# Attention scores from split operands: three rounded products in place of one full-precision product, with the rotation reordered by head

## The chip, the cores and the metric

The kernel runs on one core of one Trainium2 chip. The metric is the device time of one execution in microseconds (us). The engines have the names of the profile: PE is TensorE (matmuls), PEld its weight loads, DVE is VectorE, ACT is ScalarE, POOL is GpSimd, SP is SyncE, which starts most DMA transfers.

## The reference

Two transformer layers over x of shape (2, 1024, 256), in float32. The first layer begins with an attention, and only that stage is touched by the change:

```python
q = einsum('btd,hdk->bhtk', x, wq)            # likewise k, v; 2 heads of 128
q = fractional_rope(q, 10000.0)               # first 64 of 128 features are rotated
k = fractional_rope(k, 10000.0)               # the other 64 are kept as they are
q = q * DH ** (-0.5); k = k * DH ** (-0.5)
s = einsum('bhik,bhjk->bhij', q, k)
s = s - 1e+30 * less(i, j)                    # causal
p = softmax(s, axis=-1)
o = einsum('bhij,bhjv->bihv', p, v)
x = x + einsum('bto,od->btd', o.reshape(b, t, NH * DH), wo)
```

The x that goes into q, k and v is first multiplied by a matrix that depends on the batch entry (a weighted sum of 8 matrices under a mask). After the attention come a gated MLP with a chosen expert, a routed layer of 8 experts, and a second layer of MLPs, a gated scan and a last feed-forward layer. These take the span from about 170 us to its end.

## The kernel before

**Tiling.** The 2048 tokens are four chunks of 512 (`CH`). Chunks 0 and 1 are batch entry 0, chunks 2 and 3 are entry 1. For each chunk and head there are four query tiles of 128. Query tile i of an even chunk sees (i + 1) * 128 keys, one of an odd chunk 512 more, so the scores (`S`) are 128 to 1024 wide. In this text S(c,h,i) is the score unit of chunk c, head h, tile i, and likewise T, PV and so on.

**Split operands.** Most products of the kernel are made of three matmuls on rounded operands: a number is kept as `hi` (rounded by a cast to fp32r, mostly by ACT) and `lo` (the difference, mostly by DVE), and hi times hi, hi times lo and lo times hi are added up in PSUM (`products`, L1110 to 1116). The attention's scores (L1190), transposes (L1197) and products with the values (L1206) are exceptions: they run on plain float32 operands.

**The order of the work** is written out by `plan()`: generators append units to one list for each engine, `weave` takes a step of one generator for each step of another, and every engine runs its list in that order. One step of `advance` puts on PE the transposes T of the tile before last, then the score S of a new tile, and after odd tiles the product with the values PV. Around it the other engines run a chain for each tile: DVE's largest value `max` (L1801), ACT's `exp` (L1497), DVE's `recip` (L1806), POOL's `norm` (L2170), PE's T (L1197) and ACT's copy `p_col` (L1506). Beside it runs the preparation of the next chunk, `rotated("k", c)`, `rotated("q", c)` and `value_tiles(c)`:

- `same` (PE, 6 matmuls): the half that is rotated; `same_in` (ACT, L1470) takes it out of PSUM; `swap` (SP, two DMAs) exchanges neighbouring partitions
- `kept` (PE, 6 matmuls): the half that is kept; `skip` (ACT, L1479 and 1480) copies it with its bias to the keys `kT` or queries `qT`, half the partitions for each head
- `cosines`, `sines` (DVE, L1784, L1787), then the sum of both: head 1's 64 partitions by DVE (`rope_1`, L1796), head 0's by POOL (`rope_0`, L2164)
- `v` (PE, two times 12 matmuls) and `v_row` (ACT, L1485)

In chunk 0's stretch DVE also builds the conditioned matrix of batch entry 1 (`half`, L1759, and `half_mask`, L1762), on which the `fold` products (L1160) wait, and behind it POOL issues the indirect loads of the next stage (`ld_pack0`). In chunk 1's stretch the output product of chunk 0 (`out`) is followed by `resid` (DVE, L1815), `x1_hi` (ACT, L1521) and `x1_lo` (DVE, L1819).

**Banks.** PSUM has eight banks. Scores use banks 0 to 3, transposes 4 and 5, and same, kept, v, PV, fold and out take turns on a ring of 2 or 3 banks (6, 7 and sometimes 3). A unit waits until the previous tenant of its bank was read; the table `FREED` says by whom. For `kept` that is ACT's `skip`.

The scores before:

```python
                for w in ("k", "q"):
                    pe.wait_ge(*ready("rope_0", w, c))
                    pe.wait_ge(*ready("rope_1", w, c))
                    pe.wait_ge(*ready("skip", w, c))
                for n0 in range(0, width, CH):
                    n1 = min(n0 + CH, width)
                    pe.matmul(o[:, n0:n1], qT[c % 2][:, h, qs], kT[c // CPB][:, h, n0:n1], start=True, stop=(n1 < width))
                pe.matmul(o[:, width - P:width], ident16[:, :], causal[:, :], start=False, stop=True).then_inc(done)
```

## Time and profile before

| | us |
|---|---|
| median of 3 runs | 930.07 |
| lowest, highest | 929.25, 931.79 |
| profiled execution, whole | 926.78 |
| profiled execution, span of the profile | 925.5 |
| PE busy, share of the span | 911.2, 98% |
| DVE, ACT, POOL busy | 528.7, 444.4, 269.8 |

The rows come from one profiled execution; its own time is 1.28 us longer than the span that the rows cover and 3.3 us below the median. A timeline row is: start in us from the span's beginning, duration in us, engine, line, operation, written tile <- read tiles, size, count and, in brackets, the idle time before it with what ended it. A matmul's duration is its way through the engine, and several are under way at a time, so what one costs PE is the distance between the starts of two, and that is how the prediction reads them. A float32 score matmul has two records. The attention lies between about 29 and 170 us.

### The profile page before, as it was taken

The page shows a single profiled execution, that of the slowest core. Times are in us where ns is not written, and L with a number is a line of the kernel's source. Part 1 is how long each engine was busy: PE and PEld are TensorE (multiplying, and loading weights), DVE is VectorE, ACT ScalarE, POOL GpSimd, SP SyncE. Part 2 cuts the span into 40 slices and gives each one's busy share as a digit, 9 for nine tenths or more (in the row PEclk, how much of TensorE's full clock was granted, in tenths as well). Part 3 has the DMA queues.
Part 4 walks back from the last instruction along what each step waited for, and adds up shares of the span by engine and source line. Part 5 has one row for each costly group of instructions (what it writes and reads, how often), then busy time and mean ns, then how long its engine had stood idle before and what let it go on. Part 6 is the DMA issues. An engine that isn't in the chain of part 4 may idle for free.

```text
span 925.5 us, 13114 instructions
## 1 busy us (share of the span) xinstructions
PE 911.2 (98%) x4859; PEld 767.9 (83%) x4859; DVE 528.7 (57%) x975; ACT 444.4 (48%) x827; POOL 269.8 (29%) x242
## 2 busy tenths in 40 slices
PE   8999999999999999999999999999999999999998
PEld 4768868887799999998888888888888888888886
DVE  6754454578757766785665564333333335688544
ACT  3665566434355455572343343343343442345775
POOL 1533321310475765653400152041140230010000
PEclk9999999999999999999999999999999999999999
DMA  8030001220445343432503013003003011000011
GB/s 301 30 114 23 24 1 69 104 81 28 121 129 157 125 126 126 126 125 77 180 18 148 12 24 137 0 1 137 1 8 129 1 55 83 1 0 1 1 46 46
DMA packets 22192, 67.47 MB, mean 73 GB/s; under 512 B 4514, under 2 KB 11954, under 8 KB 19314
## 3 DMA queue, kind: packets, MB, share of 16 engines
q1 hardware_dynamic: 16546, 40.15, 11.9%
q0 software_dynamic: 5440, 26.50, 9.9%
q8 instruction: 39, 0.64, 0.3%
q14 instruction: 23, 0.19, 0.1%
q10 hardware_dynamic: 144, 0.00, 0.0%
HBM read 55.09 MB, written 9.45 MB: 70 GB/s over the span
## 4 chain that ended last, share of the span: by engine, by line
PE 89%; DVE 4%; issue 2%; DMA 2%; ACT 2%; POOL 1%; SPq 0%; ACTq 0%; DVEq 0%; POOLq 0%
PE banks L1112 18%; PE banks L1114 18%; PE banks L1113 18%; PE banks L1365 5%; PE banks L1367 5%; PE banks L1366 5%; PE banks L1206 3%; PE banks L1190 3%; PE banks L1404 2%; PE banks L1403 2%; PE banks L1197 2%; PE banks L1417 1%; PE banks L1416 1%; PE banks L1160 1%; DMA weight_stage<-in_cond_w 1%
## 5 line engine op out<-in xcount | busy, mean ns | idle before, releaser
L1112 PE MATMUL banks<-input_hi,mlp_hi 128*128 128x512 f32 x376 | 147.6, 392 | 0.0
L1114 PE MATMUL banks<-input_hi,mlp_lo 128*128 128x512 f32 x376 | 146.4, 389 | 0.0
L1113 PE MATMUL banks<-input_lo,mlp_hi 128*128 128x512 f32 x376 | 146.4, 389 | 0.0
L1631 ACT CAST hidden_hi<-hidden 128x512 fp32r<-128x512 f32 x96 | 59.6, 621 | 158.6 <-DVE hidden L2048 107.5
L2237 POOL TENSOR_TENSOR mlp_lo<-weight_stage,mlp_hi 128x768 fp32r<-128x768 f32 x32 | 59.1, 1846 | 172.4 <-ACT mlp_hi L1609 172.4
L2054 DVE TENSOR_TENSOR hidden_lo<-hidden,hidden_hi 128x512 fp32r<-128x512 f32 x96 | 66.4, 692 | 61.7 <-ACT hidden_hi L1631 61.4
L2048 DVE SCALAR_TENSOR_TENSOR hidden<-banks,L_expert_weight,gelu 128x512 f32<-128x512 f32 x64 | 48.0, 750 | 83.6 <-PE banks L1114 80.5
L1625 ACT ACTIVATE gelu<-banks 128x512 f32<-128x512 f32 x96 | 57.4, 598 | 71.2 <-PE banks L1114 63.5
L1114 PEld LDWEIGHTS banks<-input_hi,mlp_lo 128*128 128x128 f32 x376 | 70.6, 188 | 14.8
L1113 PEld LDWEIGHTS banks<-input_lo,mlp_hi 128*128 128x128 f32 x376 | 70.6, 188 | 14.4
L1112 PEld LDWEIGHTS banks<-input_hi,mlp_hi 128*128 128x128 f32 x376 | 70.6, 188 | 14.2
L1112 PE MATMUL banks<-expert_in_hi,ffn_w_hi 128*128 128x256 f32 (+1 forms) x256 | 79.8, 312 | 0.1
L1114 PE MATMUL banks<-expert_in_hi,ffn_w_lo 128*128 128x256 f32 (+1 forms) x256 | 78.9, 308 | 0.0
L1113 PE MATMUL banks<-expert_in_lo,ffn_w_hi 128*128 128x256 f32 (+1 forms) x256 | 78.8, 308 | 0.0
L1365 PE MATMUL banks<-hidden_hi,mlp_hi 128*128 128x512 f32 x192 | 75.1, 391 | 0.0
L1367 PE MATMUL banks<-hidden_hi,mlp_lo 128*128 128x512 f32 x192 | 74.8, 390 | 0.0
L1366 PE MATMUL banks<-hidden_lo,mlp_hi 128*128 128x512 f32 x192 | 74.7, 389 | 0.0
L2197 POOL TENSOR_TENSOR ffn_w_lo<-weight_stage,ffn_w_hi 128x512 fp32r<-128x512 f32 x42 | 54.5, 1300 | 32.5 <-ACT ffn_w_hi L1568 32.5
L1975 DVE TENSOR_TENSOR expert_hidden_lo<-hidden,expert_hidden_hi 128x256 fp32r<-128x256 f32 (+1 forms) x64 | 46.1, 720 | 25.9 <-ACT expert_hidden_hi L1587 25.2
L2209 POOL DMA_INDIRECT gathered<-routed_input,token_of_slot x40 | 39.7, 992 | 69.5 <-DMA routed_input<-x_rows 53.3
L2050 DVE TENSOR_TENSOR hidden<-banks,gelu 128x512 f32<-128x512 f32 x32 | 22.1, 691 | 48.4 <-PE banks L1114 48.1
L1112 PEld LDWEIGHTS banks<-expert_in_hi,ffn_w_hi 128*128 128x128 f32 x256 | 48.4, 189 | 0.7 <-issue 0.6
(350 smaller groups left out, 2148.8 us busy)
## 6 DMA issues: line engine op xcount, KB each, us to landing
weight_stage<-in_packF SPq DMA_DIRECT2D x8, 1536.0 KB, 7.0
weight_stage<-in_shared SPq DMA_DIRECT2D x2, 3072.0 KB, 11.2
expert_output<-y_rows SPq DMA_DIRECT2D x40, 128.0 KB, 1.8
weight_stage<-in_cond_w SPq DMA_DIRECT2D x4, 512.0 KB, 5.3
residual<-in_xT SPq DMA_DIRECT2D x4, 512.0 KB, 10.7
first_half_swapped<-first_half SPq DMA_DIRECT2D x16, 128.0 KB, 2.0
routed_input<-x_rows SPq DMA_DIRECT2D x16, 128.0 KB, 1.7
weight_stage<-in_ffn_w SPq DMA_DIRECT2D x2, 1024.0 KB, 7.1
```

The lines of the kernel that those rows point to most:

```text
L1112: pe.matmul(o, wh, dh, start=(i == 0), stop=False)
L1113: pe.matmul(o, wh, dl, start=False, stop=False)
L1114: last = pe.matmul(o, wl, dh, start=False, stop=(i == len(terms) - 1))
L1365: pe.matmul(o, dh[:, i, ms], hiD[r][:, :], start=first, stop=False)
L1366: pe.matmul(o, dh[:, i, ms], loD[r][:, :], start=False, stop=False)
L1367: last = pe.matmul(o, dl[:, i, ms], hiD[r][:, :], start=False, stop=final)
L1625: act.activation(gelu_t[n % 2][:, :], bank(("gu", *key, 0)), ACT.Gelu_apprx_tanh, bias=0.0).then_inc(done)
L1631: act.copy(hiD[n % 4][:, :], prod_t[n % 2][:, :]).then_inc(done)
L2048: dve.scalar_tensor_tensor(prod_t[m % 2][:, :], o, wsel[:, n // 3, n % 3:n % 3 + 1], gelu_t[m % 2][:, :], ALU.mult, ALU.mult).then_inc(done)
L2054: dve.tensor_tensor(loD[m % 4][:, :], prod_t[m % 2][:, :], f(hiD[m % 4][:, :]), ALU.subtract).then_inc(done)
L2197: pool.tensor_tensor(lo, src, f(hi), ALU.subtract).then_inc(done)
L2237: pool.tensor_tensor(wDl[s][:, qs], stage[:, qs], f((wDh if n else wDl)[s][:, qs]), ALU.subtract).then_inc(done)
```

## The change

It touches only the attention, in four ways.

1. **Scores.** Keys and queries are kept as hi and lo (`kH`, `kL`, `qH`, `qL`), and each score is three matmuls on rounded operands for each chunk of keys: q_hi with k_hi, q_hi with k_lo, q_lo with k_hi. In the chunk of the diagonal each is at least 256 wide. The first matmul waits only for the hi parts (`turn_hi`, `skip`), the second for the lo parts.
2. **Splitting.** `rope_1` (DVE) now adds all 128 partitions in place, in `cos_t`. `turn_hi` (ACT, two for each of the eight key or query units, 64 x 512) rounds it, and the rest is made by POOL for one head (`rope_0`, now a subtraction) and by DVE for the other (`rope_lo`). `skip` (ACT) writes the hi of the kept half, `skip_lo` (DVE, two for each unit, 64 x 512, reads PSUM) its lo, and a bank of `kept` is now free only after the second `skip_lo`.
3. **Slots.** Keys and values are held for three chunks in turn and not for all four; the matrices that the fold reads share memory with what `ld_pack0` loads, which therefore has three more waits.
4. **Order.** `rotated(c)` treats keys and queries in overlapping steps, each operation one step behind its input; the first `same` of chunk 1 stands ahead of S(0,0,0), the values' copies of chunk 0 stand behind the rotation on ACT, and `later_input(3)` comes after `rotated(2)`.

```diff
@@ -184,29 +185,71 @@
     def first_rotated():
         for w in ("q", "k"):
             product("out", "kept", w, 0)
-            act.append(("skip", w, 0))
-        run(value_tiles(0))
         for w in ("k", "q"):
             dve.append(("sines", w, 0))
+            dve.append(("rope_1", w, 0))
             pool.append(("rope_0", w, 0))
-        for w in ("k", "q"):
-            dve.append(("rope_1", w, 0))
-
-    def rotated(w, c):
+        for h in range(NH):
+            for w in ("q", "k"):
+                act.append(("skip", w, 0, h))
+                act.append(("turn_hi", "k" if w == "q" else "q", 0, h))
+                dve.append(("skip_lo", w, 0, h))
+            dve.append(("rope_lo", "k" if h else "q", 0))
+        run(value_tiles(0))
+
+    in_bank = []
+
+    def swapped(w, c):
         product("out", "same", w, c)
         act.append(("same_in", w, c))
         sp.append(("swap", w, c))
-        yield
+
+    def kept(w, c):
         product("out", "kept", w, c)
-        act.append(("skip", w, c))
+        for h in range(NH):
+            act.append(("skip", w, c, h))
         dve.append(("cosines", w, c))
-        yield
-        if c == 1:
-            yield
+        in_bank.append((w, c))
+
+    def rest_of_kept():
+        while in_bank:
+            unit = in_bank.pop()
+            for h in range(NH):
+                dve.append(("skip_lo", *unit, h))
+
+    def turning(w, c):
         dve.append(("sines", w, c))
         dve.append(("rope_1", w, c))
+
+    def rests(w, c):
+        dve.append(("rope_lo", w, c))
         pool.append(("rope_0", w, c))
-        yield
+
+    def rotated(c):
+        swapped("k", c)
+        yield
+        swapped("q", c)
+        yield
+        kept("k", c)
+        yield
+        rest_of_kept()
+        turning("k", c)
+        kept("q", c)
+        yield
+        rest_of_kept()
+        for h in range(NH):
+            act.append(("turn_hi", "k", c, h))
+        turning("q", c)
+        yield
+        rests("k", c)
+        for h in range(NH):
+            act.append(("turn_hi", "q", c, h))
+        yield
+        tiles_left = value_tiles(c)
+        next(tiles_left)
+        rests("q", c)
+        yield
+        yield from tiles_left
 
...
                 project.append(u[0])
             yield
         for c in chunks:
+            rest_of_kept()
             project.pop(0)
             product("out", "out", c, 0)
...
@@ -301,14 +345,16 @@
     act.append(("wo_hi",))
     pool.append(("wo_lo",))
     share_banks(False)
-    run(weave(weave(attention(0), chain(rotated("k", 1), rotated("q", 1), value_tiles(1))), chain([None] * 3, conditioned_half(4, G))))
+    coming = rotated(1)
+    next(coming)
+    run(weave(weave(attention(0), coming), chain([None] * 3, conditioned_half(4, G))))
     dve.append(("half_mask",))
     pool.append(("ld_pack0", 0))
     share_banks(True)
     fold = folded(1)
-    run(weave(attention(1), chain(some(fold, 2), later_input(2), fold, later_input(3), rotated("k", 2), rotated("q", 2), value_tiles(2))))
+    run(weave(attention(1), chain(some(fold, 2), later_input(2), fold, rotated(2), later_input(3))))
     share_banks(False)
-    run(weave(attention(2), chain(rotated("k", 3), rotated("q", 3), value_tiles(3))))
+    run(weave(attention(2), rotated(3)))
     share_banks(True)
     run(weave(attention(3), split0(0), 3))
...
@@ -783,6 +829,8 @@
         return ("gelu1" if key[2] == 0 else "prod2", *key[:2])
     if kind == "inv":
         return ("slots",)
+    if kind == "kept":
+        return ("skip_lo", *key, NH - 1)
...
+    qH = [sb("queries_hi", [P, NH, CH], F32R) for _ in range(2)]
+    qL = [sb("queries_lo", [P, NH, CH], F32R) for _ in range(2)]
+    second = sb("values", [P, QT, D])
     scored_top = top[0]
-    vR.append(sb("values", [P, TPB, D]))
+    vR = [sb("values", [P, QT, D]), second, sb("values", [P, QT, D])]
     ptT = [sb("probT", [P, TPB, PAIR]) for _ in range(2)]
-    woS, woH, woL = sb("out_weights", [P, KD, D]), sb("out_weights_hi", [P, KD, D], F32R), sb("out_weights_lo", [P, KD, D], F32R)
...
                 for w in ("k", "q"):
-                    pe.wait_ge(*ready("rope_0", w, c))
-                    pe.wait_ge(*ready("rope_1", w, c))
-                    pe.wait_ge(*ready("skip", w, c))
-                for n0 in range(0, width, CH):
-                    n1 = min(n0 + CH, width)
-                    pe.matmul(o[:, n0:n1], qT[c % 2][:, h, qs], kT[c // CPB][:, h, n0:n1], start=True, stop=(n1 < width))
+                    pe.wait_ge(*ready("turn_hi", w, c, h))
+                    pe.wait_ge(*ready("skip", w, c, h))
+                spans = [(c - 1, 0, CH)] if c % CPB else []
+                spans.append((c, width - (i + 1) * P, max((i + 1) * P, PAIR)))
+                q_hi, q_lo = qH[c % 2][:, h, qs], qL[c % 2][:, h, qs]
+                for of, n0, n in spans:
+                    pe.matmul(o[:, n0:n0 + n], q_hi, kH[of % SLOTS][:, h, 0:n], start=True, stop=False)
+                    if of == spans[0][0]:
+                        for w in ("k", "q"):
+                            pe.wait_ge(*ready("rope_0" if h == head_of_pool(w, c) else "rope_lo", w, c))
+                            pe.wait_ge(*ready("skip_lo", w, c, h))
+                    pe.matmul(o[:, n0:n0 + n], q_hi, kL[of % SLOTS][:, h, 0:n], start=False, stop=False)
+                    pe.matmul(o[:, n0:n0 + n], q_lo, kH[of % SLOTS][:, h, 0:n], start=False, stop=(of != c))
                 pe.matmul(o[:, width - P:width], ident16[:, :], causal[:, :], start=False, stop=True).then_inc(done)
             elif kind == "T":
...
-                w, c = key
+                w, c, h = key
                 o, bs = bank(("kept", w, c)), fbias[:, 1:2] if w == "q" else fbias[:, 3:4]
-                if w == "q" and c >= 2:
+                if w == "q" and c >= 2 or c >= SLOTS:
                     act.wait_ge(*ready("S", c - 2, NH - 1, QT - 1))
                 act.wait_ge(*ready("bias_in"))
                 act.wait_ge(*ready("kept", w, c))
-                dst = qT[c % 2][:, :, :] if w == "q" else kT[c // CPB][:, :, sl(c % CPB)]
-                act.activation(dst[0:P // 2, 1, :], o[0:P // 2, :], ACT.Identity, bias=bs[0:P // 2, :])
-                act.activation(dst[P // 2:P, 0, :], o[P // 2:P, :], ACT.Identity, bias=bs[P // 2:P, :]).then_inc(done)
+                dst, _ = turned_halves(w, c)
+                act.activation(dst[kept_rows(h), h, :], o[kept_rows(h), :], ACT.Identity, bias=bs[kept_rows(h), :]).then_inc(done)
+            elif kind == "turn_hi":
+                w, c, h = key
+                n = rope_no[w, c] % 2
+                if w == "q" and c >= 2 or c >= SLOTS:
+                    act.wait_ge(*ready("S", c - 2, NH - 1, QT - 1))
+                act.wait_ge(*ready("rope_1", w, c))
+                dst, _ = turned_halves(w, c)
...
                 n = rope_no[w, c] % 2
-                if w == "q" and c >= 2:
-                    dve.wait_ge(*ready("S", c - 2, NH - 1, QT - 1))
                 dve.wait_ge(*ready("cosines", w, c))
                 dve.wait_ge(*ready("sines", w, c))
-                dst = qT[c % 2][:, :, :] if w == "q" else kT[c // CPB][:, :, sl(c % CPB)]
-                dve.tensor_tensor(dst[P // 2:P, 1, :], cos_t[n][P // 2:P, :], sin_t[n][P // 2:P, :], ALU.add).then_inc(done)
+                dve.tensor_tensor(cos_t[n][:, :], cos_t[n][:, :], sin_t[n][:, :], ALU.add).then_inc(done)
+            elif kind == "skip_lo":
+                w, c, h = key
+                o, bs = bank(("kept", w, c)), fbias[:, 1:2] if w == "q" else fbias[:, 3:4]
+                hi, lo = turned_halves(w, c)
+                rs = kept_rows(h)
+                dve.wait_ge(*ready("skip", w, c, h))
+                dve.scalar_tensor_tensor(lo[rs, h, :], o[rs, :], bs[rs, :], f(hi[rs, h, :]), ALU.add, ALU.subtract).then_inc(done)
+            elif kind == "rope_lo":
+                w, c = key
+                n, h = rope_no[w, c] % 2, 1 - head_of_pool(w, c)
+                hi, lo = turned_halves(w, c)
+                rs = turned_rows(h)
+                dve.wait_ge(*ready("turn_hi", w, c, h))
+                dve.tensor_tensor(lo[rs, h, :], cos_t[n][rs, :], f(hi[rs, h, :]), ALU.subtract).then_inc(done)
...
@@ -2156,12 +2247,15 @@
             elif kind == "rope_0":
                 w, c = key
                 n = rope_no[w, c] % 2
-                if w == "q" and c >= 2:
-                    pool.wait_ge(*ready("S", c - 2, NH - 1, QT - 1))
-                pool.wait_ge(*ready("cosines", w, c))
-                pool.wait_ge(*ready("sines", w, c))
-                dst = qT[c % 2][:, :, :] if w == "q" else kT[c // CPB][:, :, sl(c % CPB)]
-                pool.tensor_tensor(dst[0:P // 2, 0, :], cos_t[n][0:P // 2, :], sin_t[n][0:P // 2, :], ALU.add).then_inc(done)
+                hi, lo = turned_halves(w, c)
+                h = head_of_pool(w, c)
+                rs = turned_rows(h)
+                pool.wait_ge(*ready("turn_hi", w, c, h))
+                if h:
+                    pool.wait_ge(*ready("rope_0", "k", 0))
+                pool.tensor_tensor(lo[rs, h, :], cos_t[n][rs, :], f(hi[rs, h, :]), ALU.subtract).then_inc(done)
+                if h:
+                    pool.wait_ge(*ready("rope_0", w, c))
...
@@ -2172,6 +2266,9 @@
                 pool.wait_ge(*ready("pick0"))
                 pool.wait_ge(*ready("cw"))
                 pool.wait_ge(*ready("half_mask"))
+                pool.wait_ge(*ready("bias_in"))
+                pool.wait_ge(*ready("fold", 0, KD - 1, 1))
+                pool.wait_ge(*ready("wo_lo"))
                 for b in range(B):
                     pool.indirect_dma_start(by_row[b][:, :], None, A["down_by_row"], bass.IndirectOffsetOnAxis(ap=dyn0[:, b:b + 1], axis=0)).then_inc(ld["by_row"], 16)
                 pool.indirect_dma_start(stage[:, 0:PK0], None, A["pack0"], bass.IndirectOffsetOnAxis(ap=dyn0[:, 0:1], axis=0)).then_inc(ld["pack0_0"], 16)
```

DVE's list in chunk 0's stretch, between the third score's `max` and the next. Names: softmax_stats is what `max` and `recip` write, times_cos and times_sin what `cosines` and `sines` write. Before, from `recip` of tile 0 on:

```order
L1806 RECIPROCAL softmax_stats_117<-softmax_stats_117 128x1
L1784 TENSOR_TENSOR times_cos_95<-first_half_91,rope_cos_89 128x512
L1801 TENSOR_REDUCE softmax_stats_117<-banks 128x1
L1806 RECIPROCAL softmax_stats_117<-softmax_stats_117 128x1
L1801 TENSOR_REDUCE softmax_stats_117<-banks 128x1
L1806 RECIPROCAL softmax_stats_117<-softmax_stats_117 128x1
L1787 TENSOR_TENSOR times_sin_97<-first_half_swapped_93,rope_sin_90 128x512
L1796 TENSOR_TENSOR keys_103<-times_cos_95,times_sin_97 64x512
```

In the change, from the same place:

```order
L1897 RECIPROCAL softmax_stats_120<-softmax_stats_120 128x1
L1864 TENSOR_TENSOR times_cos_95<-first_half_91,rope_cos_89 128x512
L1892 TENSOR_REDUCE softmax_stats_120<-banks 128x1
L1897 RECIPROCAL softmax_stats_120<-softmax_stats_120 128x1
L1880 SCALAR_TENSOR_TENSOR keys_lo_104<-banks,folded_bias_118,keys_hi_101 64x512 x2
L1867 TENSOR_TENSOR times_sin_97<-first_half_swapped_93,rope_sin_90 128x512
L1873 TENSOR_TENSOR times_cos_95<-times_cos_95,times_sin_97 128x512
L1864 TENSOR_TENSOR times_cos_96<-first_half_92,rope_cos_89 128x512
L1892 TENSOR_REDUCE softmax_stats_120<-banks 128x1
L1897 RECIPROCAL softmax_stats_120<-softmax_stats_120 128x1
```

Before, `max` of tile 3 and `recip` of tile 2 (the second TENSOR_REDUCE and the third RECIPROCAL) stood directly behind `recip` of tile 1; now five rotation operations (two `skip_lo`, `sines`, `rope_1`, `cosines`) stand between them.

PE's list in chunk 1's stretch, around the score S(1,1,1) with its 768 keys. Before (L1197 are the transposes, L1190 the score, L1206 is PV(1,0,1)):

```order
L1197 MATMUL banks<-identity_55,weight_stage_54 128x128 x7
L1190 MATMUL banks<-keys_103,queries_106 128x512
L1190 MATMUL banks<-keys_103,queries_106 128x256
L1191 MATMUL banks<-causal_mask_57,identity_bf_8_56 128x128
L1206 MATMUL banks<-probT_109,values_107 128x256 x5
L1206 MATMUL banks<-probT_109,values_107 128x128
```

In the change:

```order
L1269 MATMUL banks<-identity_55,weight_stage_54 128x128 x7
L1256 MATMUL banks<-keys_hi_100,queries_hi_107 128x512
L1261 MATMUL banks<-keys_lo_103,queries_hi_107 128x512
L1262 MATMUL banks<-keys_hi_100,queries_lo_109 128x512
L1256 MATMUL banks<-keys_hi_101,queries_hi_107 128x256
L1261 MATMUL banks<-keys_lo_104,queries_hi_107 128x256
```

Two float32 matmuls have become six rounded ones (the sixth and the causal mask follow), and behind them `kept` of the next queries now comes ahead of PV(1,0,1), which takes the bank that `kept` of the keys has filled.

## Rows read from the trace of the kernel before

**Rows 1.** The page: busy time by engine; the granted clock of PE in 40 slices.
```profile
PE 911.2 (98%) x4859; PEld 767.9 (83%) x4859; DVE 528.7 (57%) x975; ACT 444.4 (48%) x827; POOL 269.8 (29%) x242
...
PEclk9999999999999999999999999999999999999999
```
**Rows 2.** Windows: busy us (x instructions) of PE, PEld, DVE, ACT, POOL; clock; DMA.
```profile
29.40:49.90 20.50, 19.25 (x103) 14.37 (x103) 13.85 (x29) 13.15 (x34) 10.17 (x10) 1.00 0.07 26
49.90:92.00 42.10, 41.53 (x202) 30.67 (x203) 22.31 (x37) 25.56 (x51) 14.99 (x14) 1.00 0.22 76
```
**Rows 3.** Timeline of PE: T(0,0,2), the first fold, out of chunk 0, a T of chunk 3.
```profile
37.54 0.49 PE L1197 MATMUL banks<-identity,weight_stage 128*128 128x128 f32 x3
...
49.90 1.53 PE L1160 MATMUL banks<-ery_key_value_weights,cond_weight 128*128 128x384 f32 x4 [0.64 <-DVE cond_weight L1762]
...
69.00 0.50 PE L1112 MATMUL banks<-input_hi,out_weights_hi 128*128 128x512 f32 x1 [0.43 <-ACT first_half L1470]
...
125.21 0.33 PE L1197 MATMUL banks<-identity,probabilities 128*128 128x128 f32 x1 [0.34 <-ACT probT L1506]
```
**Rows 4.** Timeline of PE: scores and the causal mask behind them, 128, 640, 1024 keys.
```profile
90.81 0.39 PE L1190 MATMUL banks<-keys,queries 128*128 128x128 f32 x2
91.04 0.22 PE L1191 MATMUL banks<-causal_mask,identity_bf 128*128 128x128 bf16 x1
...
118.66 1.32 PE L1190 MATMUL banks<-keys,queries 128*128 128x512 f32 x4
119.81 0.22 PE L1191 MATMUL banks<-causal_mask,identity_bf 128*128 128x128 bf16 x1
...
141.42 1.88 PE L1190 MATMUL banks<-keys,queries 128*128 128x512 f32 x4
143.14 0.22 PE L1191 MATMUL banks<-causal_mask,identity_bf 128*128 128x128 bf16 x1
```
**Rows 5.** Timeline of PE: products of rounded operands behind PV, 512 and 256 wide.
```profile
76.33 0.48 PE L1112 MATMUL banks<-input_hi,folded_hi 128*128 128x512 f32 x1
76.64 0.39 PE L1113 MATMUL banks<-input_lo,folded_hi 128*128 128x512 f32 x1
76.87 0.39 PE L1114 MATMUL banks<-input_hi,folded_lo 128*128 128x512 f32 x1
...
87.20 0.36 PE L1176 MATMUL banks<-folded_hi,input_hi 128*128 128x256 f32 x1
87.41 0.28 PE L1177 MATMUL banks<-folded_lo,input_hi 128*128 128x256 f32 x1
87.52 0.28 PE L1178 MATMUL banks<-folded_hi,input_lo 128*128 128x256 f32 x1
```
**Rows 6.** Timeline of DVE: the rotation of chunk 0, a reciprocal, the mask.
```profile
24.46 1.28 DVE L1787 TENSOR_TENSOR times_sin<-first_half_swapped,rope_sin 128x512 f32<-128x512 f32 x2
...
27.36 1.78 DVE L1796 TENSOR_TENSOR queries<-times_cos,times_sin 64x512 f32<-64x512 f32 x1
...
35.66 0.15 DVE L1806 RECIPROCAL softmax_stats<-softmax_stats 128x1 f32<-128x1 f32 x1
...
49.07 0.68 DVE L1762 TENSOR_TENSOR cond_weight<-cond_weight,cond_mask 128x512 f32<-128x512 f32 x1
```
**Rows 7.** Timeline of POOL: the rotation of chunk 0's queries.
```profile
26.85 1.73 POOL L2164 TENSOR_TENSOR queries<-times_cos,times_sin 64x512 f32<-64x512 f32 x1
```
**Rows 8.** Groups by form, DVE, 29 to 147 us: a sum that reads PSUM.
```profile
L1815 DVE TENSOR_TENSOR residual<-banks,residual 128x512 f32<-128x512 f32 x6 | 4.2, 692 | 4.6 <-PE banks L1114 4.6
```
**Rows 9.** Timeline of ACT: `skip` of a head, a rounding copy from SBUF.
```profile
24.90 0.68 ACT L1479 ACTIVATE queries<-banks,folded_bias 64x512 f32<-64x512 f32 x1 [0.95 <-PE banks L1114]
...
29.83 0.62 ACT L1455 CAST out_weights_hi<-out_weights 128x512 fp32r<-128x512 f32 x1
```
**Rows 10.** Timeline of ACT and DVE: `x1_hi` and `x1_lo` of chunk 0.
```profile
71.42 1.05 ACT L1521 CAST input_hi<-residual 128x1024 fp32r<-128x1024 f32 x1 [2.47 <-DVE residual L1815]
```
```profile
72.50 1.23 DVE L1819 TENSOR_TENSOR input_lo<-residual,input_hi 128x1024 fp32r<-128x1024 f32 x1 [1.11 <-ACT input_hi L1521]
```

38 lines of the change are left out of this document (26 added, 12 removed).

## The prediction

> **What bounds the kernel now.** I read the page first: PE is busy for 98% of the span, and the granted clock is full in all forty slices [rows 1], so nothing is to be had from the clock (the rows read here lie on its level of 2.4 GHz), and a microsecond of PE work removed is a microsecond of time, as long as nobody lets PE wait. The attention has that form too, but less safely. In chunk 0's stretch, 29.4 to 49.9 us, PE is busy for 19.25 of 20.5 us and DVE for 13.85; from 49.9 to 92 it is 41.53 and 22.31 of 42.1 [rows 2]. DVE is thus the next engine in chunk 0, with 6.65 us of slack, and that slack lies in small gaps. Of PE's waits the ones that matter are 0.64 us before the first fold, for DVE's mask, 0.43 us before the output of chunk 0, and 0.34 us before a transpose in chunk 3 [rows 3]. From 170 us on the change touches nothing; what comes there starts from what PE has finished, so I let it shift as a whole.
>
> **PE work.** A score costs from its first record to the causal mask behind it: 0.23 us for 128 keys, 1.15 for 640, 1.72 for 1024 [rows 4]. That is about 0.21 us for each 128 keys on a full 512 (0.86), and 0.23 for the first. So four tiles of an even chunk and head cost about 0.23 + 0.43 + 0.65 + 0.86 = 2.17 us, and of an odd one 1.15 + 1.34 + 1.53 + 1.72 = 5.74 us. The new scores are the same kind of matmul as the split products: 0.23 us from start to start at 512 columns and 0.11 to 0.12 at 256, but the first of a group that follows float32 work costs 0.31 and 0.21 [rows 5]. In nearly all cases a transpose or a PV stands ahead of a score, so I charge each score one dear first matmul, and 0.17 for each 384-wide one. Even: 0.45 twice (the 128-key tile is 256 wide now), 0.60, 0.77, together 2.27 us, which is 0.10 more than before. Odd: 0.77 for the old chunk each time, plus 0.36, 0.36, 0.51, 0.69, together 5.00 us, which is 0.74 less. Each kind comes four times (two chunks, two heads). The odd chunks give back 3.0 us, chunk 2 costs 0.2, and chunk 0's 0.2 is inside the next term.
>
> The Trainium skill has a rule on this ("FP8 and Floating Point Precision", TensorE Precision Notes): true FP32 goes through the array four times, reduced precision once. By that three passes replace four. Read with this kernel's rows it would give a quarter of the scores' 4 * (2.17 + 5.74) = 31.6 us, that is 7.9 us; the rows say 2.6 us net, because of the 256 minimum and the dear first matmul. The sum goes by the rows.
>
> **Chunk 0: DVE.** Ahead of S(0,0,0) DVE does two sines and two sums from 24.46 to 29.14 us; the sums take 1.78 us beside POOL's [rows 6, 7]. It now does two sines (1.28), two sums over all partitions that mostly miss POOL (about 0.7 each), four `skip_lo` and two `rope_lo`. The trace has no `skip_lo`; between a sine's 0.64 and 1.78 us I take 0.69, the addition that reads PSUM [rows 8]. A `rope_lo` reads two tiles of SBUF beside POOL's subtraction: between 0.64 and 1.78 I take 1.0. That is 1.3 + 1.4 + 2.8 + 2.0 = 7.5 us, so DVE gets to its first `max` at about 32.0 in place of 29.1. PE does not idle for that, since `same` of chunk 1 (1.4 us) now stands ahead and S(0,0,0) starts at about 30.4. In the stretch itself DVE gets four more `skip_lo` and two more `rope_lo`, 4.8 us. 32.0 + 13.85 + 4.8 gives 50.7 us for the end of the mask if DVE never waits, against 49.75 (49.07 + 0.68) [rows 6]: 0.9 us late at least. It will wait: the second `max` needs S(0,0,1), the cosines need ACT's `same_in`, the `skip_lo` need ACT's `skip`. And the order makes PE wait too. `recip` of tile 2, done at 35.8 before [rows 6], now stands behind `max` of tile 3 and that behind two `skip_lo`, sines, a sum and cosines, 3.3 us of work that starts at about 35.7. With POOL's `norm` behind it T(0,0,2), at 37.54 before [rows 3], comes at about 40.5, and PE stands for some 3 us, the largest new gap I expect. Walking the lists on with these durations, the mask ends at 51.3 to 52.5 and the first fold starts 2.2 us later than its 49.90. Bounds: 0.9 us if DVE is never kept waiting, 5 us if it can use only half of its 6.65 us of slack (4.8 + 2.9 of added work and delay less 3.3, and 0.6 for contention).
>
> The Trainium skill tells where such contention ends ("SBUF — State Buffer", Who interferes with whom): a DVE instruction with two SBUF inputs blocks against a POOL instruction that reads SBUF, one with a single SBUF input does not. The trace agrees on the sums (1.78 beside 1.73 us of POOL, 0.64 for a sine alone). By it `skip_lo` is safe and the sums, `half` and `rope_lo` are not.
>
> **ACT.** Sixteen `turn_hi` of about 0.62 us [rows 9]; `skip` keeps its 0.68 each. In chunk 0's stretch ACT rises from 13.15 by 2.5 of 20.5 us [rows 2], and ahead of it by another 2.5, which delays the values' copies, the exp of tile 0 and POOL's `wo_lo`. PE would wait for that only where it already waits for DVE, so it costs nothing of its own; its cover is DVE's lateness, and without that it would cost up to 1 us.
>
> **Chunk 1: the bank.** PV(1,0,1) takes the bank of `kept` of the keys, which was free after ACT's `skip` and now is free after DVE's second `skip_lo`. From the end of `out`: the residual's sum 0.69, `x1_lo` after `x1_hi` 1.05 + 1.23, cosines 0.64, the `max` of S(1,1,1) about 1, two `skip_lo` 1.4: DVE frees it after some 6.2 us [rows 8, 10]. PE needs it after `kept`, seven transposes, S(1,1,1) and `kept` of the queries, 1.4 + 0.8 + 1.1 + 1.4 = 4.7 us. That is a wait of up to 1.5 us; I take 1.4. On the other side the 0.43 us before `out` [rows 3] goes, since `same` of the queries now gives ACT time. Net +1.0. Bounds: -0.4 (DVE gets there in time) and +2.
>
> **Chunks 2 and 3.** Chunk 2's new DVE work (six operations, 4.8 us) lies beside long PE work (four rotation products, two of values, two of `out`), and the bank is needed only at `v`; nothing. In chunk 3 a T waited 0.34 us for the softmax chain [rows 3], which does not get shorter, while PE gets there sooner. Of the 1.5 us that chunk 3 gives, I let 0.4 be lost (bounds 0 and 0.8).
>
> **Other moves, at nothing.** SP's swaps keep their number, and the later ones have whole PE products to land in. POOL has as many operations as before; its `rope_0` of the keys stands one `norm` later. `ld_pack0` waits in addition for things that are done before the mask, but as the mask is late, its three issues are too, and the `norm` behind them; that is inside the 2.2 us. The slots' waits are on scores and PVs of two chunks ago, done long before.
>
> **The sum**: -3.0 + 0.2 + 2.2 + 1.0 + 0.4 = +0.8 us. The profiled execution would go from 926.8 to 927.6; it stands 3.3 us below the median, so 930.07 becomes 930.9.
>
> **The rivals.** A change of 0.3%, 2.8 us, is about what a measurement of this kernel can tell from none.
>
> - *Faster: the overlap does what it is for.* DVE's gaps are filled, the first fold comes 0.9 us late at most, no bank wait: -3.0 + 0.2 + 0.9 - 0.4 = -2.3 us. With the dear first matmul hidden as well, because the weights of the next are loaded under the scores' long ones (0.08 us for each of 32 scores, 2.6 us), -4.9, 925.2 us. For it: ordinary spacing of 0.23 inside a group. Against: the rows behind PV, and T before nearly each score. A quarter off the scores, as by the page, would be 922 us before waits.
> - *Slower: DVE and POOL block each other in chunk 0.* The sums, `half` and `rope_lo` each wait for a POOL subtraction of 1.7 us, the mask ends 5 us late, the folds and the loads with it, and chunk 1 adds its 2 us: -2.8 + 5 + 2 + 0.8 = +5, 935 us. It decides from the point where DVE has under 2 us of idle left between 29 and 50 us. For it: the 1.78 us row; against: the subtractions are on 64 partitions as before and no more numerous.
> - *The scores are not cheaper at all* (each of the three matmuls as dear as half a float32 one): 1.5 times 31.6 is 16 us more. The rows for the same kind of operands exclude it nearly; 2%.
>
> **Chances.** My forecast with its bounds, 0.5; the faster rival past 0.3%, 0.23; the slower one past 0.3%, 0.27, which includes the last. Leaving out 2 in 10, the range is 926.0 to 936.0.
>
> **What would show it.** PE's busy time falls by 2 to 4 us, with a score of 1024 keys at 1.46 us from start to mask and one of 128 keys at 0.45. A gap of 2 to 4 us before T(0,0,2) near 38 us, released by POOL. The first fold at 51 to 53 us, released by DVE's mask. A gap of about 1 us before PV(1,0,1). From 170 us on all stretches as long as before. Wrong it would be if the first fold starts before 50.5 or after 54 us, if the score of 1024 keys takes 1.72 us, or if the part behind 170 us changes its length by over 1 us.

## The result and the profile after

The changed kernel takes 940.54 us (median of 4 executions, 939.83 to 942.43), the kernel before 930.93 us beside it (929.25 to 932.46): a ratio of 1.0107, 95% interval 1.0088 to 1.0126. Repeated later beside others it was 1.0097 (1.0080 to 1.0113). I had forecast 930.9 us in a range of 926.0 to 936.0. The change costs 9 to 10 us.

The page, busy time by engine, answers to [rows 1]: PE's work rose by 3.6 us though the scores got cheaper, since part of it runs at a lower clock; in a second profile of the same kernel, at full clock, it is 910.1 us, 1.1 less than before.

```profile
PE 914.8 (97%) x4907; PEld 779.0 (83%) x4907; DVE 543.8 (58%) x999; ACT 452.6 (48%) x843; POOL 266.5 (28%) x242
```

Windows of the changed kernel, columns as in [rows 2]; the first ends, as there, at the first fold. The stretch of chunk 0 is 25.78 us long and not 20.5; PE is idle for 4.4 us of it, and DVE works 22.41 us. The next has 3.7 us of idle PE.

```profile
29.40:55.18 25.78, 21.36 (x121) 17.67 (x119) 22.41 (x40) 18.40 (x43) 10.91 (x12) 0.93 0.06 22
55.18:97.40 42.22, 38.54 (x201) 30.74 (x202) 25.60 (x40) 25.15 (x49) 13.64 (x13) 1.00 0.22 75
```

The timeline of PE, the larger waits up to chunk 3 (in brackets the idle time and its releaser). They answer to [rows 3], where the largest is 0.64 us.

```profile
42.43 0.52 PE L1269 MATMUL banks<-identity,weight_stage 128*128 128x128 f32 x3 [2.76 <-POOL weight_stage L2264]
...
55.18 0.56 PE L1225 MATMUL banks<-ery_key_value_weights,cond_weight 128*128 128x384 f32 x1 [0.18 <-DVE cond_weight L1842]
...
69.78 0.49 PE L1177 MATMUL banks<-input_hi,folded_hi 128*128 128x512 f32 x1 [1.08 <-DVE folded_lo L1851]
...
83.62 2.65 PE L1278 MATMUL banks<-probT,values 128*128 128x256 f32 x12 [1.55 <-DVE keys_lo L1880]
...
100.84 0.47 PE L1177 MATMUL banks<-input_hi,folded_hi 128*128 128x512 f32 x1 [1.85 <-issue]
...
121.36 0.47 PE L1177 MATMUL banks<-input_hi,out_weights_hi 128*128 128x512 f32 x1 [1.66 <-DVE times_cos L1873]
...
137.75 0.33 PE L1269 MATMUL banks<-identity,probabilities 128*128 128x128 f32 x1 [0.61 <-ACT probT L1586]
```

In order these are T(0,0,2), the first fold, `same k 2`, PV(1,0,1), `same k 3`, `out 1 0` and a T of chunk 3. With four of 0.4 to 0.55 us between 32 and 61 us and one of 0.41 before values at 96.21, PE's waits up to chunk 3 come to some 12 us, against some 3 before.

The scores themselves, to be held against [rows 4]: 1024 keys from 89.37 to the mask at 90.84, 1.47 us; 128 keys from 98.32 to 98.76, 0.44 us.

```profile
89.37 0.47 PE L1256 MATMUL banks<-keys_hi,queries_hi 128*128 128x512 f32 x1
...
90.84 0.23 PE L1263 MATMUL banks<-causal_mask,identity_bf 128*128 128x128 bf16 x1
...
98.32 0.36 PE L1256 MATMUL banks<-keys_hi,queries_hi 128*128 128x256 f32 x1
...
98.76 0.23 PE L1263 MATMUL banks<-causal_mask,identity_bf 128*128 128x128 bf16 x1
```

Why T(0,0,2) waits is told by DVE's timeline and POOL's (rows of POOL behind them). The scores of tile 2 are long there, but `recip` of tile 2 stands behind `skip_lo` of k 1 (L1880), sines, a sum, cosines and the `max` of tile 3, as forecast, and is done at 41.6, where it was 35.8 before [rows 6].

```profile
37.40 1.53 DVE L1880 SCALAR_TENSOR_TENSOR keys_lo<-banks,folded_bias,keys_hi 64x512 fp32r<-64x512 f32 x2
38.86 0.67 DVE L1867 TENSOR_TENSOR times_sin<-first_half_swapped,rope_sin 128x512 f32<-128x512 f32 x1
39.64 0.69 DVE L1873 TENSOR_TENSOR times_cos<-times_cos,times_sin 128x512 f32<-128x512 f32 x1
40.24 0.69 DVE L1864 TENSOR_TENSOR times_cos<-first_half,rope_cos 128x512 f32<-128x512 f32 x1
40.85 0.68 DVE L1892 TENSOR_REDUCE softmax_stats<-banks 128x1 f32<-128x512 f32 x1
41.45 0.15 DVE L1897 RECIPROCAL softmax_stats<-softmax_stats 128x1 f32<-128x1 f32 x1
```
```profile
41.70 0.58 POOL L2264 TENSOR_SCALAR weight_stage<-weight_stage,softmax_stats 128x384 f32<-128x384 f32 x1 [3.76 <-DVE softmax_stats L1897]
```

The new work of DVE by form, 22 to 125 us (count | busy us, mean ns). Of the low parts, `skip_lo` is L1880 and `rope_lo` L1887: 12.0 and 8.3 us. POOL's sums of before are gone from the path, and DVE's sum over all partitions (0.69 us) misses POOL.

```profile
L1880 DVE SCALAR_TENSOR_TENSOR queries_lo<-banks,folded_bias,queries_hi 64x512 fp32r<-64x512 f32 x8 | 6.0, 750 | 0.3
L1880 DVE SCALAR_TENSOR_TENSOR keys_lo<-banks,folded_bias,keys_hi 64x512 fp32r<-64x512 f32 x8 | 6.0, 749 | 0.2
L1873 DVE TENSOR_TENSOR times_cos<-times_cos,times_sin 128x512 f32<-128x512 f32 x8 | 5.5, 692 | 0.8
L1887 DVE TENSOR_TENSOR queries_lo<-times_cos,queries_hi 64x512 fp32r<-64x512 f32 x4 | 4.6, 1150 | 0.2
...
L1887 DVE TENSOR_TENSOR keys_lo<-times_cos,keys_hi 64x512 fp32r<-64x512 f32 x4 | 3.7, 922 | 0.1
```

### The profile page after: what moved, and what is told of

The parts are those of the page before. It is cut to its first block, busy times and chain, and to the rows that moved or that the text cites. A ratio compares the mean times of both kernels' runs of the same rounds, so it can differ in the third digit from the quotient of the medians.

```text
span 941.2 us, 13294 instructions
## 1 busy us (share of the span) xinstructions
PE 914.8 (97%) x4907; PEld 779.0 (83%) x4907; DVE 543.8 (58%) x999; ACT 452.6 (48%) x843; POOL 266.5 (28%) x242
## 4 chain that ended last, share of the span: by engine, by line
PE 88%; DVE 6%; issue 2%; ACT 2%; DMA 1%; POOL 0%; SPq 0%; DVEq 0%; ACTq 0%; POOLq 0%
PE banks L1177 19%; PE banks L1179 19%; PE banks L1178 19%; PE banks L1437 5%; PE banks L1439 5%; PE banks L1438 5%; PE banks L1278 2%; PE banks L1476 2%; PE banks L1475 2%; PE banks L1488 1%; PE banks L1489 1%; PE banks L1269 1%; PE banks L1353 1%; DMA weight_stage<-in_cond_w 1%; DVE softmax_stats L1892 1%
## 5 line engine op out<-in xcount | busy, mean ns | idle before, releaser
L2066 DVE TENSOR_TENSOR expert_hidden_lo<-hidden,expert_hidden_hi 128x256 fp32r<-128x256 f32 (+1 forms) x64 | 44.2, 691 | 26.3 <-ACT expert_hidden_hi L1667 24.6
```

## The experiments

Three theories stood after the result: single steps stand in the wrong place (**order**); the low parts' work is too much for DVE (**work**); PE's lower granted clock behind the waits (**clock**). Each ratio below is to the kernel before, measured beside it with five rounds; 0.001 is 0.93 us, and the intervals reach 0.001 to 0.002 to either side.

**The changed kernel again.**

> The changed kernel itself, beside the others of this group, since the kernel before took 926.97 us beside the last four and 930.93 beside the first measurement. Expected: the same ratio as first measured, 1.0107 within its interval of 1.0088 to 1.0126.

1.0097. Its profile has the same waits at the same places, but the clock stays full (windows of PE: busy, clock, DMA; first this run, then the changed kernel as first profiled).

```profile
40.00:50.00 10.00, 7.09 (x49) 1.00 0.00 1
100.00:110.00 10.00, 9.93 (x56) 1.00 0.15 55
```
```profile
40.00:50.00 10.00, 7.57 (x46) 0.83 0.00 1
100.00:110.00 10.00, 9.16 (x40) 0.83 0.15 53
```

In the first profile matmuls at half the rate follow the wait of 2.76 us at 42.43 and that of 1.85 us at 100.84, which puts them on the 1.2 GHz level for a while; here the same waits have nothing behind them. Between T(0,0,2) and the first fold both profiles take the same 12.7 us (42.43 to 55.18, 41.68 to 54.42), because PE here stands 1.24 us for POOL at 48.63 instead. Between `same k 3` and `out 1 0` it is 20.52 against 18.90 us: there the clock costs 1.6 us. The six executions of this run took 937.02 and 938.18 us at a mean granted clock of 1.000, 937.78 at 0.998, and 939.24 to 941.28 at 0.994 to 0.995; but one of the first measurement took 940.25 at 1.000. So the lower clock has a part in the ratios, of a size that was not isolated.

```profile
48.63 0.30 PE L1269 MATMUL banks<-identity,probabilities 128*128 128x128 f32 x1 [1.24 <-POOL probabilities L2264]
...
118.97 0.47 PE L1177 MATMUL banks<-input_hi,out_weights_hi 128*128 128x512 f32 x1 [1.69 <-DVE times_cos L1873]
```

A measure of the attention alone is the time from the first `kept` product of chunk 0 to the last `out` product that reads the high parts of both operands. Here are the two rows before, then those of this run, both at full clock: 145.35 and 154.34 us, 9.0 us more. The first profile of the changed kernel, with its lower clock, has 156.00.

```profile
22.98 0.69 PE L1112 MATMUL banks<-input_hi,folded_hi 128*128 128x512 f32 x1
...
168.33 0.39 PE L1112 MATMUL banks<-input_hi,out_weights_hi 128*128 128x512 f32 x1
```
```profile
23.28 0.69 PE L1177 MATMUL banks<-input_hi,folded_hi 128*128 128x512 f32 x1
...
177.62 0.39 PE L1177 MATMUL banks<-input_hi,out_weights_hi 128*128 128x512 f32 x1
```

What lies behind the last `out` does not go with the kernel but with the group of runs, each group having been made on a chip of its own: 756.2 to 757.7 us in the eight profiles of two groups, 759.3 to 761.5 in the seven of the other two. The medians of the kernel before differ likewise, 925.96 and 926.97 us against 930.27 and 931.38. Spans of single profiles from different chips can thus differ by some 4 us without any change.

**Order: the input of chunk 3 early.**

```
-    run(weave(attention(1), chain(some(fold, 2), later_input(2), fold, rotated(2), later_input(3))))
+    run(weave(attention(1), chain(some(fold, 2), later_input(2), fold, later_input(3), rotated(2))))
```

> Of the changed kernel, one move is undone: in the stretch of chunk 1 the input of chunk 3 is made ahead of the rotation of chunk 2, as before the change. Theory (the move, which I had costed at nothing, makes the products of `same k 3` wait for `x0_lo 3`, and TensorE then runs at its lower clock for a while): the wait of 1.85 us at 100.84 goes and most of the 10 us of lower clock behind it with it, so 2.5 to 3.5 us less than the changed kernel's 940.5: 937.0 to 938.0. Rival (the time is only moved: chunk 2's rotation is late instead, or the wait at `out 1 0` grows): 940 to 941.

1.0099, so the rival. The wait at `same k 3` is gone, and these two stand in the timeline of PE instead: the bank of `kept` of k 2 comes free later, and an `o_lo` holds the values.

```profile
84.91 0.50 PE L1177 MATMUL banks<-input_hi,folded_hi 128*128 128x512 f32 x1 [2.73 <-DVE keys_lo L1880]
...
97.54 0.39 PE L1241 MATMUL banks<-folded_hi,input_hi 128*128 128x256 f32 x1 [1.83 <-DVE input_lo L1902]
```

**Order: `recip` earlier on DVE** (a pass over DVE's finished list moves each `recip` up to two operations behind its row's `max`).

> Of the changed kernel, only VectorE's order is changed: each `recip` stands at most two other operations behind its row's `max`, instead of up to six, so that GpSimd gets its normalization earlier; no work is added or removed. Theory (in chunk 0 `recip 0 0 2` stands behind the low parts of k 1, GpSimd idles for it, and T(0,0,2) waits 2.76 us, with TensorE at its lower clock for some us behind): the wait shrinks below 1 us and the clock stays, 2 to 4 us less than 940.5: 936.5 to 938.5, with the first fold at 52 to 53.5 instead of 55.18. Rival (VectorE is simply full in this stretch, so whatever is put first delays the rest): `same k 2` and the mask wait longer by what T(0,0,2) gains, 939.5 to 941.

1.0136: the rival, and more than it wanted (939.5 to 941 us, up to 1.011). T(0,0,2) waits 0.52 us, and within 12 us PE waits three times elsewhere, first for the bank of `kept` of q 1.

```profile
39.80 0.52 PE L1285 MATMUL banks<-identity,weight_stage 128*128 128x128 f32 x3 [0.52 <-POOL weight_stage L2280]
...
43.93 0.89 PE L1294 MATMUL banks<-probT,values 128*128 128x256 f32 x4 [1.60 <-DVE queries_lo L1896]
...
48.88 0.33 PE L1285 MATMUL banks<-identity,probabilities 128*128 128x128 f32 x1 [1.58 <-ACT probT L1602]
...
51.33 1.04 PE L1294 MATMUL banks<-probT,values 128*128 128x256 f32 x3 [1.21 <-ACT values L1581]
```

**Order: `o_lo 1 1 3` first.**

```
+    dve.remove(("o_lo", 1, 1, 3))
+    dve.insert(dve.index(("sines", "q", 3)), ("o_lo", 1, 1, 3))
```

> The changed kernel with one operation of VectorE moved: `o_lo 1 1 3` stands ahead of `sines q 3` and `rope_1 q 3`, not behind them. Theory (`out 1 0` waits 1.69 us because its last input stands two operations behind, and nothing hides it): 1.2 to 1.5 us less than the changed kernel, ratio 1.0082, with the wait at `out 1 0` under 0.5 us. Rival (the rotation of q 3 is late in its place, or a later wait takes it back): 1.0097, as the changed kernel.

1.0111. `out 1 0` follows after 0.24 us, and the values behind it wait for ACT, whose copy stands behind `turn_hi` of the rotation that is now later: 1.07 of the 1.69 us come back. That the ratio is no lower than 1.0097 is within the intervals.

```profile
117.60 0.47 PE L1179 MATMUL banks<-input_hi,out_weights_hi 128*128 128x512 f32 x1 [0.24 <-issue]
...
121.65 0.39 PE L1243 MATMUL banks<-folded_hi,input_hi 128*128 128x256 f32 x1 [1.07 <-ACT values L1567]
```

**Both repairs.**

> The changed kernel with both single repairs that keep its result: the input of chunk 3 ahead of chunk 2's rotation, and `o_lo 1 1 3` ahead of `sines q 3`. Each alone left the time where it was (1.0099 and 1.0111 against 1.0097 and 1.0107). Theory (VectorE's total work up to the end of chunk 2's stretch decides, so a repaired wait comes back at the next place): 1.008 to 1.011. Rival (the waits are separate, and the two repairs save 1.9 and 1.7 us together): 1.006 or less.

1.0096: they do not add up.

**Order: the old one, and other work moved out of chunk 0.** In the first, k and q are rotated one after the other as before, with `turn_hi` and the rests one step behind. In the second, the last four `half` and the mask go behind `later_input(2)` and `later_input(3)` into chunk 1.

> The new arithmetic in the old order: k and q of a chunk are rotated one after the other, as before the change, no rotation is begun ahead of the attention loop, and the input of chunk 3 is early; of the change's own order only this stays, that the high and low parts are formed one step behind the products of the rotation. Theory that the new order is at fault: under 936. Theory that the split's own work on VectorE and GpSimd is at fault in chunk 0, in whatever order: 937 to 942, without the wait for the input of chunk 3.

> Of the changed kernel, work that is not the split's is moved out of the full stretch: the last four `half` steps and the mask of the second folded weights (five operations of VectorE) are made beside chunk 1 and not beside chunk 0, the inputs of chunks 2 and 3 ahead of the fold; nothing is added or removed. Theory (VectorE is too full between 30 and 60 us, and has room between 60 and 80): the waits at PV(1,0,1) and `same k 3` shrink, 3 to 6 us less than the changed kernel: ratio 1.004 to 1.008. Rival (chunk 2's rotation, now one step later, is late for chunk 2's scores): 1.010 or more, with a wait of some us at S(2,0,0).

1.0155 and 1.0150. The first is above both theories (under 936 us, or 937 to 942, which is up to 1.012): in the old order PE waits 3.40 us for POOL's `norm` at 49.26 and 3.09 us before `out 1 0` at 123.77. The new order is thus the better one for the new arithmetic. The second falls as a remedy: T(0,0,2) waits 2.76 us as before, since the `half` steps stand behind it, and where the fold was there is now a wait of 3.20 us for the softmax chain; the folds had been PE's cover. Chunk 2's first score also waits, 0.81 and 0.98 us, which is the rival's sign. That DVE has room later was right and no help.

**Clock: filler at T(0,0,2).**

```
+    spin(10, 4)
+    pe.insert(pe.index(("T", 0, 0, 2, 0)), pe.pop())
```

> The changed kernel with ten filler products (bf16, 512 columns, about 2.1 us together, result not used) on TensorE ahead of T(0,0,2), where it waits 2.76 us. Theory (the wait itself costs 2.76 us, and the lower clock behind it another 1.5; the filler takes away only the second): granted clock 1.00 between 40 and 50 us, 1.3 to 1.7 us less than the changed kernel, ratio about 1.009. Rival (the lower clock there is not owed to the wait, or what TensorE loses there it would have waited anyway): the same as the changed kernel.

1.0122: nothing gained, the rival. The clock is at 1.00 from 40 to 50 us, as it also is in some profiles without filler; what was lost there PE would have waited. This prices the clock at one place only: the four executions with the filler still have a mean clock of 0.996 to 0.998.

**Work: the low parts left out, or formed and not read.** Edits: no `skip_lo`, `rope_lo`, `rope_0` in the lists; or only this in the scores:

```
-                q_hi, q_lo = qH[c % 2][:, h, qs], qL[c % 2][:, h, qs]
+                q_hi, q_lo = qH[c % 2][:, h, qs], qH[c % 2][:, h, qs]
...
-                    pe.matmul(o[:, n0:n0 + n], q_hi, kL[of % SLOTS][:, h, 0:n], start=False, stop=False)
+                    pe.matmul(o[:, n0:n0 + n], q_hi, kH[of % SLOTS][:, h, 0:n], start=False, stop=False)
```

> Of the changed kernel, the low parts of the rotated queries and keys are left out (VectorE's `skip_lo` and `rope_lo`, GpSimd's `rope_0`); the three products stay, all of them on the high parts, so TensorE's work is the same and the scores lack the two correction products' content. Theory (what the split costs is its additional work on VectorE and GpSimd, and the waits that this makes): waits at T(0,0,2), PV(1,0,1) and `out 1 0` go, that for the input of chunk 3 stays with its lower clock (3.5 us): 930.9 - 2.8 + 3.5 = 931.6, within 930 to 934. Rival (the three products themselves are dearer than priced somewhere, or the order of the steps is at fault and not the work): 937 or more.

> The low parts are formed as in the changed kernel, with the same work on VectorE and GpSimd, and they free the banks as there; but the scores' three products all read the high parts, so the scores lack the correction products' content and TensorE waits for no low part. Leaving the low parts out altogether gave 1.0025 of the kernel before. Theory (the cost is that the work fills VectorE in chunk 0 and holds what stands behind it, recips, banks, `o_lo`): 1.009 to 1.012, as the changed kernel. Rival (the cost is that TensorE waits for the low parts to be ready): 1.002 to 1.005.

1.0025 (1.0014 to 1.0035) and 1.0122 (1.0107 to 1.0136). This pair decides: the loss comes with the work, and it stays whole when nobody reads the result. Of the attention alone, at full clock, the profiles say the same: 145.23 us without low parts, 154.20 with low parts that nobody reads, 154.34 with all as changed. (That 1.0122 is above 1.0097 is thus not found in the attention; the intervals overlap.) In this order PE does not wait for low parts, it waits for what stands behind them; in two of the reordered kernels above a score did wait for POOL's low part, 0.87 us in the old order and 0.98 with the `half` steps moved. The rows, without low parts and then with unread ones:

```profile
23.30 0.69 PE L1171 MATMUL banks<-input_hi,folded_hi 128*128 128x512 f32 x1
...
168.53 0.39 PE L1171 MATMUL banks<-input_hi,out_weights_hi 128*128 128x512 f32 x1
```
```profile
23.23 0.69 PE L1177 MATMUL banks<-input_hi,folded_hi 128*128 128x512 f32 x1
...
177.43 0.39 PE L1177 MATMUL banks<-input_hi,out_weights_hi 128*128 128x512 f32 x1
```

**Which part of the work.**

> As the kernel that forms the low parts and does not read them (1.0122 of the kernel before; the changed kernel itself 1.0097), but without `skip_lo`, the low parts of the rows that are not rotated: four VectorE operations of 0.76 us in each chunk, which also hold the bank of `kept`. The scores again lack the correction products' content. Leaving out all low parts gave 1.0025. Theory (it is VectorE's time and the held bank): `skip_lo` has the larger part, about 3.1 of 5.3 us in a chunk, so two thirds of the 0.0075 to 0.0097 go: 1.004 to 1.006. Rival (the cost is GpSimd's `rope_0` and what VectorE loses beside it): 1.008 to 1.010.

> The other half alone: `skip_lo` stays, and `rope_lo` (VectorE, 0.69 us) and `rope_0` (GpSimd, 1.29 us), the low parts of the rotated rows, are left out; nothing reads low parts. Theory (VectorE's time and the held bank): a third goes, 1.007 to 1.009. Rival (GpSimd's share and the contention, where a VectorE operation of 0.67 us takes 1.6 to 1.7 beside it): 1.003 to 1.005.

1.0033 and 1.0088. `skip_lo` carries 8.3 us of the difference to 1.0122 (6.0 us of that to 1.0097), more than its share of the time and more than forecast; the rotated rows' low parts carry 1 to 3 us, POOL's operations among them. The two do not simply add up: taken out one at a time they give 8.3 and 3.2 us, together 9.0. Without `skip_lo` the attention takes 146.66 us at full clock, 7.5 less than the 154.20, and without the rest too it takes another 1.4 less.

```profile
23.64 0.69 PE L1174 MATMUL banks<-input_hi,folded_hi 128*128 128x512 f32 x1
...
170.30 0.39 PE L1174 MATMUL banks<-input_hi,out_weights_hi 128*128 128x512 f32 x1
```

**`skip_lo`: its time, or the bank it holds.**

```
-  lo[rs, h, :], o[rs, :], bs[rs, :], f(hi[rs, h, :])
+  lo[rs, h, :], ropeC[rs, sl(c % CPB)], bs[rs, :], f(hi[rs, h, :])     (bank free after skip)
+  lo[rs, h, 0:1], o[rs, 0:1], bs[rs, :], f(hi[rs, h, 0:1])             (bank as before)
```

> As the kernel that forms the low parts and does not read them, but `skip_lo` takes its first operand from a table in SBUF (wrong values, same size, same place in the order) and the bank of `kept` is free once `skip` has read it. Theory (VectorE's time, what stands behind it in its queue): as with the bank held, 1.009 to 1.012. Rival (the held bank, by which PV(1,0,1) waits 1.55 us and others with it): 1.5 to 3 us less, 1.006 to 1.008.

> As the kernel that forms the low parts and does not read them, but `skip_lo` works on one column and not on 512: it stands in the same place and frees the bank of `kept` at the same point of VectorE's order, and takes a small part of its 0.75 us. Theory (VectorE's time is the cost): close to the kernel without `skip_lo`, 1.003 to 1.005. Rival (the bank held until VectorE comes to it is the cost): 1.007 to 1.010.

The first, 1.0134, is inconclusive: with both operands in SBUF `skip_lo` took 0.93 us and not 0.75, which adds nearly 3 us of DVE work; the wait at PV(1,0,1) is gone there, but T(0,0,2) waits 4.20 us. The second, 1.0044, speaks for DVE's time: the same places in the queue and the same bank, but 0.22 us each, and most of the cost is gone. The wait at PV(1,0,1) falls from 1.55 to 0.49 us with it, so it is mostly that time seen at a bank. What the held bank would cost by itself was not isolated, since DVE also comes to it sooner here. DVE by form, 22 to 125 us:

```profile
L1879 DVE SCALAR_TENSOR_TENSOR queries_lo<-banks,folded_bias,queries_hi 64x1 fp32r<-64x1 f32 x8 | 1.7, 217 | 0.3
```

**What is left without low parts.**

> The kernel without any low parts (1.0025 in the new order) in the old order of the steps, with the input of chunk 3 early; the scores lack the correction products' content. Theory (the new order costs some 4 us by itself, for T(0,0,2) waits 1.8 us, `same k 3` 1.85 and `same k 2` 1.08 there although no low part is made; what is left is the 2.8 us that TensorE saves): 0.997 to 0.999. Rival (the waits come from the additional high parts on ScalarE, in whatever order): 1.002 to 1.005.

1.0022 (1.0010 to 1.0034), where the order theory wanted 0.999 or less: by its number the rival. Without low parts both orders are thus 2 us slower than before, though their scores are cheaper: summed over the 32 scores, from first record to causal mask, they take 31.5 us before and 29.1 us without low parts. But the granted clock is not the same on both sides, a third explanation beside order and high parts. Without low parts it is 0.996 to 0.999 in the new order and 0.994 to 0.998 in the old one, while the kernel before beside them has 0.999 to 1.000 and 0.996 to 1.000. In the new order the execution with the highest clock took 926.48 us, below the 926.97 of the kernel before; the other seven took 928.19 to 929.68. Its attention, all at full clock, takes 145.23 us against 145.35. There the waits, 1.81 us at T(0,0,2), 1.08 at `same k 2` and 1.85 at `same k 3` among them, use up the 2.4 us of the scores and no more; the further 2 us of the ratio may be the clock's, which was not tested. In the old order the waits are released by ACT's high parts and the chain behind them; from 50 to 60 us its granted clock is 0.66.

```profile
51.22 0.48 PE L1244 MATMUL banks<-keys_hi,queries_hi 128*128 128x512 f32 x1 [1.92 <-ACT queries_hi L1546]
...
53.37 0.98 PE L1213 MATMUL banks<-ery_key_value_weights,cond_weight 128*128 128x384 f32 x1 [0.78 <-DVE cond_weight L1829]
```

The releasers point to the sixteen `turn_hi` on ACT (0.61 us each); what they cost by themselves was not tried. No version with the right scores beat the kernel before.

## Why the prediction was wrong

The prediction had the change at +0.8 us. At full clock the attention grew by 9.0 us: 4.2 us up to the first fold, where 2.2 were forecast, and 4.8 us from the first fold to the last `out` (118.43 to 123.20 us), where -1.4 was. What failed is the pricing of DVE's added work: at 2.2 us in chunk 0, and at nothing behind it except for one bank.

- **PE work: right for a score, too high in the sum.** 1.47 and 0.44 us against 1.46 and 0.45 forecast. But the 32 scores fell from 31.5 to 29.4 us, 2.1 and not 2.6: four scores of an odd chunk cost 5.66 us before and 5.07 after, where I had 5.74 and 5.00 from interpolated rows. PE's busy time at full clock fell by 1.1 us, under the 2 to 4 that I named. The quarter off that I had read from the Trainium skill's four passes for true FP32 ("FP8 and Floating Point Precision", TensorE Precision Notes) is not seen; it is 7%.
- **"DVE gets to its first `max` ...": nearly right.** 32.9 us in the repeated profile against 32.0, and S(0,0,0) waits 0.43 us where I had none. **The gap before T(0,0,2): right.** 2.76 us, released by POOL, where I had said some 3. The durations held: `skip_lo` 0.75 (0.69 taken), `rope_lo` 0.69 alone and 0.92 to 1.15 on average (1.0 taken).
- **"The first fold starts 2.2 us later": wrong.** It starts at 55.18 against 49.90; of these 5.28 us 1.05 lie ahead of the rotation of chunk 0 (the first `kept` product at 24.03 against 22.98, a matter of the execution: 23.28 when repeated). 4.2 us are the change's. My walk let DVE catch up behind T(0,0,2); but PE and DVE wait there for each other by turns, and the next waits (1.24, 0.52, 0.50 us in the repeated profile) each add. From 29 to 50 us DVE has 2.2 us of idle left, where it had 6.9; the slower rival was to hold from under 2.
- **Chunk 1's bank: right in size,** 1.55 against 1.4 (the terms for DVE add up to 6.0 us, not to the 6.2 written), and the 0.43 us before `out` went as said; but I did not see that `folded_lo` delays `same k 2` by 1.08 us.
- **"Other moves, at nothing": wrong.** The input of chunk 3 went behind chunk 2's rotation, and the text did not even name it; `same k 3` waits 1.85 us for it (`x0_hi` on ACT at 98.43, `x0_lo` on DVE until 100.7). Undoing it gained nothing, so its true price beside the rest is near nought: the step failed in the reading of the trace, not in the sum.
- **"Chunk 2's new DVE work lies beside long PE work; nothing": wrong.** `out 1 0` waits 1.66 us, since its `o_lo` stands behind two `skip_lo`, sines (1.74 us beside POOL) and a sum. This and the last are one error: I priced DVE stage by stage by slack, while the queue carries the delay into the next stage, and each repair only moves the place where it shows. The runs put in its place a price of 12.0 us of `skip_lo` at 6 to 8 us.
- **"ACT ... costs nothing of its own ... up to 1 us": open.** Without the low parts PE's saving of 2.4 us is used up even at full clock, but order and high parts were not separated.
- **From 170 us on: no effect of the change shown.** The part behind the last `out` is 761.16 and 759.31 us in the two profiles against 757.21, more than the 1 us that I named as a sign of being wrong; but it goes with the group of runs and its chip, and so does a wait of 1.7 to 2.0 us near 266 us, which only the profiles with the longer part have.
- **The slower rival** gave 935 and put it to sums and `rope_lo` blocked by POOL. The side was right, the mechanism not: the sums miss POOL, and the rotated rows' low parts cost the least.

The account of the attention at full clock, one profile for each step: -2.4 us from the scores, +2.3 from high parts and order together, +1.4 from the low parts of the rotated rows, +7.5 from `skip_lo`, +0.1 from reading the low parts; sum +9.0 (145.35 to 154.34, the last figures rounded).

## What to carry over

Do not price work added to an in-order engine by the slack that its stretch shows. Here DVE came to work 22.4 of the 25.8 us of chunk 0's stretch, and 12 us of `skip_lo` on a queue that PE, ACT and POOL wait on cost 6 to 8 us: between half and two thirds of their duration. A wait in the timeline is where the delay shows, not what it costs: move one thing at a time on the chip before calling it a price, and leave the work out (or form it and don't read it) to find its true price. Compare single profiles only at the same granted clock, and from one chip or by a stretch that does not depend on it. To make a matmul cheaper by splitting its operands, first count who forms the parts.

## What was not expected of the hardware

- The granted clock behind a wait is not the same in each execution: the same program had 0.83 in the windows 40 to 50 and 100 to 110 us once and 1.00 in both the other time, with the same waits of 2.76 and 1.85 us ahead.
- An operation of 64 partitions and one column that reads PSUM takes 0.22 us on DVE against 0.75 us for 512 columns.
- The same operation with its PSUM operand replaced by one in SBUF got slower on average, 0.93 against 0.75 us, in a stretch where POOL works beside it.
- The same program differs from chip to chip: the kernel before had medians of 925.96, 926.97, 930.27 and 931.38 us in four groups of runs, each on another chip. In the profiles of the runs beside it most of the difference lies behind the attention.
